# Second graph layer of a graph and attention network: near products moved in between the single sums of the second and third chunk

## The reference, cut to what matters

```
xn = layernorm(x)
h_self  = xn @ W_self.T
neigh   = segment_sum(xn[src], dst) / max(degree, 1)
h_neigh = neigh @ W_neigh.T
h = h_self + h_neigh + bias
x = x + layernorm(h) * gamma + beta
```

## Time and profile before

| | us |
|---|---|
| median of three runs | 1593.94 |
| profiled execution | 1593.68 |
| its span | 1591.9 |
| stage `graph_last`, its sums, near products and turnings | 953.86 to 1041.96 |
| TensorE busy in the span | 1455.6 (91%) |
| VectorE busy | 1001.4 (63%) |
| ScalarE busy | 722.9 (45%) |

### The profile page before, as it was taken

One profiled execution on the slowest core, in us unless ns is written; L12 is line 12 of the kernel. 1 busy time (PEld: TensorE's weight loads), 2 busy tenths in 40 slices (PEclk: granted clock), 3 DMA queues, 4 the chain that ended last, 5 costly groups with the idle time before them and its releaser, 6 DMA issues. The chain is left out here.

```text
span 1591.9 us, 22269 instructions
## 1 busy us (share of the span) xinstructions
PE 1455.6 (91%) x8144; PEld 899.4 (57%) x8144; DVE 1001.4 (63%) x1877; ACT 722.9 (45%) x1406; POOL 639.1 (40%) x530
## 2 busy tenths in 40 slices
PE   4888999998888899999999899979999988998998
PEld 2554545446666754454545554546686776776664
DVE  7997254337877602123213321768999999999994
ACT  4442114335556521111111230155788787787783
POOL 4787100035656300000000043016876775776863
PEclk9999999999999899999999999989999999999999
DMA  7001000062121060000000110003011101101001
GB/s 245 1 2 83 0 1 1 0 173 61 35 61 41 1 241 0 0 0 1 0 0 0 43 38 0 1 12 82 1 36 33 34 10 26 34 2 35 1 1 65
DMA packets 28284, 55.72 MB, mean 35 GB/s; under 512 B 7872, under 2 KB 12612, under 8 KB 27920
## 3 DMA queue, kind: packets, MB, share of 16 engines
q1 hardware_dynamic: 26864, 51.71, 11.7%
q10 hardware_dynamic: 1312, 2.56, 0.4%
HBM read 28.77 MB, written 5.84 MB: 22 GB/s over the span
## 5 line engine op out<-in xcount | busy, mean ns | idle before, releaser
L1480 POOL TENSOR_TENSOR tl_ex<-tl_ex,tl_left 128x1250 f32<-128x1250 f32 x80 | 209.8, 2622 | 24.4 <-ACT tl_left L1815 19.5
L1299 DVE SCALAR_TENSOR_TENSOR X<-ex_ps_x,g,X 128x512 f32<-128x512 f32 x80 | 59.9, 751 | 192.6 <-PE ex_ps_x L1192 192.6
L656 POOL TENSOR_SCALAR ex_small<-ex_small,inv 128x128 f32<-128x128 f32 (+4 forms) x40 | 49.8, 1246 | 272.0 <-DVE inv L1028 270.7
L1984 POOL TENSOR_TENSOR lo<-xn,hi 128x512 f16<-128x512 f32 x5 | 5.9, 1187 | 374.1 <-ACT hi L2088 374.1
L1620 PE MATMUL tl_banks<-identf,tl_ex 128*128 128x128 f32 x800 | 133.8, 282 | 24.2 <-ACT tl_pt L1836 14.4
L1836 ACT COPY tl_pt<-tl_banks 128x512 f32<-128x512 f32 (+1 forms) x200 | 108.2, 541 | 90.0 <-PE tl_banks L1620 89.5
L1165 PE MATMUL ex_ps_h<-yt,w 128*128 128x512 f32 (+1 forms) x384 | 143.3, 527 | 0.0
L1192 PE MATMUL ex_ps_x<-w,hid 128*128 128x512 f32 (+1 forms) x320 | 143.1, 599 | 0.0
L1245 ACT ACTIVATE hid<-ex_ps_h,b 128x512 f32<-128x512 f32 (+1 forms) x48 | 29.1, 608 | 242.0 <-PE ex_ps_h L1165 241.9
L1620 PEld LDWEIGHTS tl_banks<-identf,tl_ex 128*128 128x128 f32 x800 | 88.5, 141 | 85.7 <-issue 44.4
L1906 DVE MAX8 tl_m<-tl_banks 128x8 f32<-128x1250 f32 x80 | 116.3, 1454 | 10.1 <-PE tl_banks L1590 9.9
(11 more groups left out here) (281 smaller groups left out, 2990.2 us busy)
## 6 DMA issues: line engine op xcount, KB each, us to landing
tl_kl<-tl_KT SPq DMA_DIRECT2D x16, 320.0 KB, 4.4
tl_qs<-tl_QO SPq DMA_DIRECT2D x16, 320.0 KB, 6.0
kl<-KT SPq DMA_DIRECT2D x14, 320.0 KB, 4.4
qs<-QO SPq DMA_DIRECT2D x14, 320.0 KB, 5.8
w<-in_L_ffn_W SPq DMA_DIRECT2D x8, 512.0 KB
w<-in_L_ffn_W SPq DMA_DIRECT2D x4, 1024.0 KB, 8.8
at_kept<-AT SPq DMA_DIRECT2D x1, 3200.0 KB, 9.0
AT<-at_kept SPq DMA_DIRECT2D x1, 3200.0 KB, 18.6
```

The costliest lines, as they stand in the source:

```text
L1480: pool.tensor_tensor(ex[:, n % EXS, 0:N], ex[:, n % EXS, 0:N], left[:, n % LEFT, :], ALU.subtract).then_inc(s_probs, 1)
```

## The change

The single sums become separate calls, and so do the copies behind them. On TensorE, the near products of the first eight tiles now stand between single sums: those of tiles 0 to 3 between the sums of chunk two, those of tiles 4 to 7 between the sums of chunk three. The turnings come behind the last single sum: two directly behind it, then the near products of tiles 8 and 9, then the ten other turnings. The lists of VectorE and ScalarE are written out in a matching order. VectorE's `scales(1)` moves from before tile 8 to behind tile 9, and `scales(0)` from behind tile 7 to behind tile 3. What is computed, and with which instructions, stays the same. GpSimd's list, the DMAs and all other layers are the same.

```diff
-            gather(0)
-            gather(1)
-            for t in range(0, 4):
+            for f in range(KD):
+                gather(0, f)
+            gather(1, 0)
+            near(0)
+            near(1)
+            gather(1, 1)
+            near(2)
+            gather(1, 2)
+            near(3)
+            gather(1, 3)
+            gather(2, 0)
+            near(4)
+            near(5)
+            gather(2, 1)
+            near(6)
+            gather(2, 2)
+            near(7)
+            gather(2, 3)
+            for v in range(2):
+                turn_next(v)
+            for t in range(8, NT):
                 near(t)
-            gather(2)
-            for t in range(4, NT):
-                near(t)
-                if t < NT - 1:
-                    turn_next(t - 4)
-            for v in range(NT - 5, 3 * KD):
+            for v in range(2, 3 * KD):
                 turn_next(v)
...
         @block.scalar
...
-            for t in range(4, 8):
-                root(t)
-                if t < 7:
-                    keep_next(t - 4)
+            keep(0, 1)
+            keep(0, 3)
+            root(0)
+            root(1)
+            keep(1, 1)
+            root(2)
+            root(3)
+            keep(1, 3)
             roots(0)
-            roots(1)
+            root(4)
+            keep(2, 1)
+            root(5)
+            root(6)
+            keep(2, 3)
+            keep_next(0)
+            keep_next(1)
+            root(7)
+            for v in range(2, 5):
+                keep_next(v)
             root(8)
-            for v in range(3, 8):
+            for v in range(5, 10):
                 keep_next(v)
             root(9)
-            for v in range(8, 3 * KD):
+            for v in range(10, 3 * KD):
                 keep_next(v)
+            roots(1)
             roots(2)
...
         @block.vector
...
+            keep(0, 0)
+            keep(0, 2)
+            keep(1, 0)
+            for t in range(0, 3):
+                tile(t)
+            keep(1, 2)
+            tile(3)
             scales(0)
+            keep(2, 0)
+            tile(4)
+            tile(5)
+            keep(2, 2)
+            for t in range(6, NT):
+                tile(t)
             scales(1)
-            for t in range(8, NT):
-                moments(t)
-                affine(t)
             scales(2)
```

More of the change, by code:

```diff
@@ L2018, in own_rows, with gather @@
                 mm.then_inc(s_own, 1)
-            def gather(c):
+            def gather(c, f):
                 a, w = CUTS[c]
[L2022 to L2033, removed]
+                if c:
+                    pe.wait_ge(s_kept_a if f % 2 else s_kept_v, 2 * (c - 1) + f // 2 + 1)
+                else:
+                    pe.wait_ge(s_w_kept, KD + f + 1)
+                for t in range(NT):
+                    if c == 0 and f == 0:
+                        pe.wait_ge(s_low_v if t % 2 else s_low_p, t // 2 + 1)
+                    for part in (hi, lo):
+                        mm = pe.matmul(ps_a[:, f, 0:w], part[:, t, f * P:(f + 1) * P], m.AT[:, t, a:a + w],
+                                       start=(t == 0 and part is hi), stop=(t == NT - 1 and part is lo))
+                mm.then_inc(s_summed, 1)
             def near(t):
@@ L2092, in keep_own, with keep @@
                 act.copy(own[:, t, :], ps_n[:, t % 2, :]).then_inc(s_own_kept, 1)
-            def keep(c):
+            def keep(c, f):
                 a, w = CUTS[c]
-                for f in (1, 3):
-                    act.wait_ge(s_summed, KD * c + f + 1)
-                    act.copy(agg[:, f, a:a + w], ps_a[:, f, 0:w]).then_inc(s_kept_a, 1)
+                act.wait_ge(s_summed, KD * c + f + 1)
+                act.copy(agg[:, f, a:a + w], ps_a[:, f, 0:w]).then_inc(s_kept_a, 1)
             def root(t):
@@ L2157, in keep_cols, with keep @@
                 dve.tensor_copy(xt[:, t % XT, :, :], ps_t[:, t % 2, :, :]).then_inc(s_cols, 1)
[L2159 removed]
+            def keep(c, f):
                 a, w = CUTS[c]
[L2161 to L2163 removed]
+                dve.wait_ge(s_summed, KD * c + f + 1)
+                dve.tensor_copy(agg[:, f, a:a + w], ps_a[:, f, 0:w]).then_inc(s_kept_v, 1)
             def moments(t):
@@ L2224, in _, with tile @@
                     keep_weight(KD + t)
-            keep(0)
-            keep(1)
-            for t in range(0, 4):
+            def tile(t):
                 moments(t)
                 affine(t)
-            keep(2)
-            for t in range(4, 8):
-                moments(t)
-                affine(t)
-            scales(0)
+            keep(0, 0)
[5 more added lines that the diff above has]
+            tile(3)
+            scales(0)
+            keep(2, 0)
[4 more added lines that the diff above has]
+                tile(t)
             scales(1)
-            for t in range(8, NT):
-                moments(t)
-                affine(t)
             scales(2)
```

5 lines of the change are left out of this document (removed).

## The result

The changed kernel takes 1597.32 us, the median of 20 runs (1593.58 to 1602.37), against 1592.22 us of 20 runs of the kernel before. The ratio is 1.0033, 95% interval 1.0024 to 1.0042: slower by 5.3 us, between 3.8 and 6.7, and less than the 0.5% named as no change. The forecast of no change held, and the time lies in the range. But the forecast's own size, +0.3 to +2.3, did not. (The prediction counted from 1593.94, the median of three runs, which lies 1.7 above that of the 20.)

A forecast was written before the change was run, and what follows sets the result against it. VectorE closes the stage, idle while TensorE sums chunks two and three. Tile 9 starting 0.02 later plus 1.02 for `scales(1)` gives +1.0, so 1594.7 profiled and 1594.9 for a median; range 1589.5 to 1600.5 us.

The forecast's parts named there:

- The forecast of no change: Whole kernel: a difference under 0.5%, 8.0 us, reads as the same; given 92%, with faster 4% and slower 4%.
- the forecast's own size: Whole kernel: the stage's later end makes the time longer by +0.3 to +2.3 us; given 70%.
- The walk: Changed stage, followed instruction by instruction on TensorE, VectorE and ScalarE at the old trace's paces; stage ends at 1043.0, not 1041.96.
- the stall: Tile 8 on VectorE: its reciprocal waits 3.67 us for ScalarE's root, which stands behind the copies of blocks 2 to 4.
- the sum: End of the stage: tile 9 starts 0.02 later and the second group's scales add 1.02, +1.0 us in all.
- The first rival: End of the stage: VectorE's whole head start of 12.95 us arrives, time 1581.0; chance 3%.
- The second rival: Tile 8 is not held, or the clock gives back most of the 1.0; -0.7, 1593.2 us; chance 15%.
- the clock behind the stage: Next layer's start: TensorE's clock is already low, so longer idle time costs nothing; transposes may give back about 0.5 us.
- the third rival: Clock falls in the turnings, stage ends 3.4 us later, 1597.3; or it rises later in the next layer; chance 12%.

The follow-up runs named there:

- e12: Changed kernel with the root of tile 8 ahead of the copies of blocks 2 to 5 on ScalarE, nothing else; 1591.41 us, a single run.
- e11: Changed kernel with the second group's scales ahead of tile 8 again on VectorE and ScalarE, nothing else; 1590.05 us, a single run.
- e1: Changed kernel run again with no edit; 1596.31 us, ratio 1.0029 to the kernel before.
- e10: Changed kernel run a third time with no edit; 1595.93 us, ratio 1.0027 to the kernel before.
- e2: Changed kernel with 36 more transposes on TensorE behind the last turning, no part of what is computed; 1592.32 us, ratio 0.9992 to the kernel before.
- e5: Kernel before with 14 more transposes on TensorE behind the last turning; 1593.12 us, ratio 1.0014 to the kernel before.
- e4: Only the near products of tiles 0 to 3 put between chunk two's sums, rest of TensorE's order as before; 1592.80 us, ratio 1.0012 to the kernel before.

## Why the prediction was right, and where it was not

**The walk.** Right in its steps, with 0.52 added to the profile's times: tile 0 at 979.08 (forecast 979.08), tile 8 at 1029.11 (1029.11), the stall 3.52 (3.67), tile 9 at 1036.79 (1036.84), the second group's scales 1.02 (1.02), TensorE without a gap up to near 9. The stage grew by 0.85 where the sum said 1.0; most of the difference is tile 9, which took 4.04 (1040.31 - 1036.27) and not the 4.16 of before. That the stall is decisive and that the scales cost their 1.02 only where they now stand is shown by e12 and e11, not only read from the order.

**The first rival** (the head start of 12.95 us arrives) was rightly given little: 3.7 us of it reach tile 8, and the stall takes them.

**The second rival** (the stall is smaller, or the clock gives back what the stage lost) did not happen. Its size without the stall was near: in e12 the stage is 1.1 under the kernel before, where it said 0.7.

**The failed step is the clock behind the stage.** The prediction said that the clock was already low when the next layer began, so that a longer idle time has nothing left to take there, and that the later start might give back 0.5. That was read from one execution. In three profiles the changed kernel pays 0.2, 0.8 and 4.6 there, the kernel before nothing. The second half of the third rival, a clock that is low for longer in the next layer, is nearest to what happened: it gave 1597.3 and 12%, and the median is 1597.32. That the two numbers meet is luck: the rival counted 3.4 from 1593.94, and the measured 5.1 count from 1592.22. It had the place in part. A lower clock over the 30 us where the next layer begins (0.72 against 0.77) is there in e1 and e10, but costs 0.9 and 1.3 us at the first search and not 3.4. The dearest low stretch, in e10, is not at the transposes ahead of 1050 but at 1070 to 1080, where VectorE's searches begin. Its first half, a fall in the turnings, did not come: the clock is at 1.00 through them in all three profiles.

**The rule on gaps.** The Trainium skill (TensorE: Matmul & The Clock Gate, Why this matters for your kernels) says that idle gaps between bursts of products bring the clock down; by it the prediction called a longer gap a risk. The gap of 5.03 is there, and filling it pays 4.0 us (e2). In the profiles the direction is borne out: 0.89 over the 30 us in all three kernels with the gap filled, 0.72 to 0.83 in the others. As a forecast of the time it is not: e5 fills the gap of before and gains nothing in the median, e11 has a gap of 4.1 at no price behind the stage, and e4 loses without a longer gap.

**What stays open.** The stage (0.85) and the mean of the three profiles behind it (1.9) make 2.7; the medians of the three sets lie 5.1, 4.0 and 3.4 over. The rest, 0.7 to 2.4 us, is in the timed executions, whose low stretches can't be placed; the 1.9 itself rests on one profile of three. Nor is it settled why the fill pays 4.0 in the changed kernel and nothing in the median of before, though both profiles show the same clock behind it. Why the order in the stage decides how often the clock is low behind it is not settled either.

## What to carry to other kernels

An engine that is started earlier gains only up to the last piece that feeds it; ask what stands ahead of that piece's partners in every other list. Here one square root of 0.3 us, written behind three copies that had to wait for TensorE, took 3.5 us of a lead of 12.95. Small pieces that were hidden in a wait (a group's scales) cost their full price once they stand behind the last wait. And where TensorE has pauses, one profile is one draw of its clock (549.8, 550.4 and 554.2 us behind the same stage): a term for it needs several profiles, or the mean granted clock of the timed runs beside the medians.

## What the runs showed of the hardware

The low clock does not need idle time right ahead of it. TensorE is busy throughout these stretches of the kernel before, far ahead of the stage; the clock falls at 700 to 710, and over the 100 us it is granted 0.97:

```profile
695.00:700.00 5.00, 5.00 (x33) 1.00 0.00 0
700.00:710.00 10.00, 10.00 (x25) 0.66 0.00 0
...
700.00:800.00 100.00, 100.00 (x250) 0.97 0.00 0
```

The unchanged code up to the first copy of a sum took between 952.9 and 961.7 us over all profiles of this study. The five profiles that are granted 0.98 from 20 to 953 us have their first copy at 952.9 to 954.7, the nine at 0.97 have it at 953.5 to 961.7. That 9 us scatter, as wide as that of the kernel's runs, is ahead of the stage, and it is why a change of 1 us in a stage can be read from a stage's length and not from a median.
